# Mixture-of-experts stage: the up-weights of each tile come by SyncE's DMA, not by a GpSimd copy

## What is computed

```python
aff = x @ centroids.T                    # 8 experts
eid = argmax(aff)                        # one expert for each token
alpha = sigmoid(sum(x * centroids[eid]))
xln = norm(x) * ln_g[eid] + ln_b[eid]
h   = relu(xln @ w1[eid] + b1[eid])      # 128 -> 512, the up-weights
y   = h @ w2[eid] + b2[eid]              # 512 -> 128, the down-weights
out = x + alpha * y                      # then x + layernorm(out)
```

## Time and profile before

| | us |
|---|---|
| runs shown | 2639.48, 2630.18, 2635.62 |
| their median | 2635.62 |
| the profiled execution, device time | 2626.78 |
| the profiled execution, span of its instructions | 2625.0 |
| mean granted TensorE clock | 0.88 |

### The profile page before, as it was taken

The page is one execution under the profiler, slowest core; times in us unless marked ns, Lnnn a source line. Parts: engine busy times, 40 slices in busy tenths (PEclk is TensorE's granted clock), DMA queues, the critical chain, the costliest instruction groups (busy, mean ns, idle before and its releaser), DMA issues. The chain is left out here.

```text
span 2625.0 us, 38988 instructions
## 1 busy us (share of the span) xinstructions
PE 1928.0 (73%) x11612; PEld 985.5 (38%) x11693; DVE 1798.8 (69%) x3789; ACT 1524.6 (58%) x2831; POOL 1166.7 (44%) x734
## 2 busy tenths in 40 slices
PE   2688888788787762988267778787877886578886
PEld 0344545455454431888122222222222221133432
DVE  5565655665655432455259999999999999756665
ACT  1576667766676531665256666666676665344453
POOL 1021212212222011466258898998999888500000
PEclk7799989998999865999689999999999888778887
DMA  3010001000010000221111121111121211001111
GB/s 136 9 29 21 25 23 37 22 21 23 24 33 17 13 21 28 59 69 57 52 45 47 49 60 45 44 44 48 49 59 49 55 41 33 25 28 40 32 40 48
DMA packets 137132, 105.23 MB, mean 40 GB/s; under 512 B 12896, under 2 KB 130832, under 8 KB 136608
## 3 DMA queue, kind: packets, MB, share of 16 engines
q1 hardware_dynamic: 131488, 89.51, 12.3%
q0 software_dynamic: 5504, 13.90, 1.5%
HBM read 42.20 MB, written 27.61 MB: 27 GB/s over the span
## 5 line engine op out<-in xcount | busy, mean ns | idle before, releaser
L1843 POOL TENSOR_TENSOR hc<-h,c_rep 128x1024 f32<-128x1024 f32 x256 | 614.4, 2418 | 102.2 <-DVE h L1804 97.4
L1804 DVE TENSOR_TENSOR_SCAN h<-decay,bank 128x1024 f32<-128x1024 f32 x256 | 572.7, 2269 | 0.0
L1689 ACT ACTIVATE decay<-bank,neg_a_r 128x510 f32<-128x510 f32 x512 | 322.8, 683 | 274.0 <-PE bank L1580 241.9
L1795 DVE TENSOR_TENSOR bank<-bank,b_rep 128x1024 f32<-128x1024 f32 x256 | 302.8, 1215 | 45.2 <-PE bank L1567 45.0
L1567 PE MATMUL bank<-u,sel_u 128*128 128x512 bf16 x489 | 166.3, 421 | 209.1 <-DVE h L1804 199.3
L664 ACT ACTIVATE es<-bank 128x384 f32<-128x384 f32 x512 | 210.9, 501 | 127.2 <-PE bank L469 127.2
L1013 POOL DMA_INDIRECT rows_in_dram<-row,idx x64 | 66.5, 1039 | 428.2 <-DVE row L956 413.5
L444 PE MATMUL bank<-xt,w_a 128*128 128x512 f32 x224 | 145.2, 743 | 66.1 <-DVE rot_b L822 31.8
L1567 PEld LDWEIGHTS bank<-u,sel_u 128*128 128x128 bf16 x512 | 32.8, 99 | 385.6 <-DVE h L1804 347.8
L1580 PE MATMUL bank<-d,sel_u 128*128 128x512 bf16 x481 | 166.8, 423 | 4.0 <-issue 1.0
L1594 PE MATMUL bank<-hc,y_sel 128*32 128x512 f32 x1024 | 142.6, 630 | 4.6 <-POOL hc L1843 4.6
(11 more groups left out here) (341 smaller groups left out, 4351.6 us busy)
## 6 DMA issues: line engine op xcount, KB each, us to landing
xvs<-xv SPq DMA_DIRECT2D x16, 512.0 KB, 3.3
xs<-rows_in_dram SPq DMA_DIRECT2D x72, 68.0 KB
w<-in_w_dram SPq DMA_DIRECT2D x2, 2048.0 KB
x_in<-in_x_dram SPq DMA_DIRECT2D x16, 256.0 KB
xlb_dram<-xl SPq DMA_DIRECT2D x16, 256.0 KB
xlb_m<-xlb_dram SPq DMA_DIRECT2D x16, 256.0 KB
x_m<-in_x_dram SPq DMA_DIRECT2D x16, 256.0 KB
g_xn<-yx_dram SPq DMA_DIRECT2D x16, 256.0 KB
```

The lines of the kernel that those rows point to most:

```text
L1689: act.activation(decay[n % 4][:, i, :, 1:], seq(DL[i])[:, :, 1:], ACT.Exp, scale=c["neg_a_r"][:, hf, g:g + 1]).then_inc(s["n_da"], 1)
L1795: dve.tensor_tensor(pair_of(BD[n % 2]), pair_of(BD[n % 2]), b_rep[p if n < NS else q][:, :].unsqueeze(1).to_broadcast([P, 2, STEP]), ALU.m ...
L1804: dve.tensor_tensor_scan(flat(h[n % 4]), decay[n % 4].rearrange("p i b t -> p (i b t)"), BD[n % 2], 0.0, ALU.mult, ALU.add).then_inc(s["n_ ...
L1843: pool.tensor_tensor(hc[n % 4][:, :, :], h[n % 4][:, :, :], c_rep[p][:, :].unsqueeze(1).to_broadcast([P, 2, STEP]), ALU.mult).then_inc(s[" ...
```

## The change

`copy` moves from GpSimd's program to SyncE's, where it is a DMA from SBUF to SBUF. The single semaphore `weights`, which GpSimd raised by 1, is replaced by four, one for each slot, raised by 16 by a DMA; TensorE waits for 16(n+1) of the slot's own. SyncE's order is new as well: the rows of pass 0, the weights of pass 0, the rows of passes 1 to 5, and then one block for each pass k with the four weights of pass k+1 (each behind its wait for `hidden`) followed by the rows of pass k+4 (behind `y2` at k-1).

```diff
@@ block.sync
-            for m in range(ROWS):
-                load(m, m)
-            with sp.Fori(0, PASSES // ROWS - 1) as n:
-                for i in range(ROWS):
-                    done = sp.snap(n * ROWS + (i + 1))
-                    sp.wait_ge(s["y2"], done)
-                    load(n * ROWS + (ROWS + i), i)
+            def copy(n, j, first):
+                t = n * SLOTS + j
+                col = sp.value_load(c["tile_col"][0:1, 0, bass.ds(t, 1)], min_val=0, max_val=(E - 1) * F)
+                if not first:
+                    done = t - (SLOTS - 1)
+                    sp.wait_ge(s["hidden"], done if isinstance(done, int) else sp.snap(done))
+                sp.dma_start(w1[j][:, :], c["w_1"][:, bass.ds(col, F)]).then_inc(weights[j], 16)
+
+            def one_pass(k, x):
+                for j in range(SLOTS):
+                    copy(k + 1, j, False)
+                if x is not None:
+                    done = k - 1
+                    sp.wait_ge(s["y2"], done if isinstance(done, int) else sp.snap(done))
+                    load(k + 4, x)
+
+            load(0, 0)
+            for j in range(SLOTS):
+                copy(0, j, True)
+            for m in range(1, ROWS):
+                load(m, m)
+            one_pass(0, None)
+            one_pass(1, None)
+            with sp.Fori(0, (PASSES - 6) // ROWS) as n:
+                for i in range(2, 2 + ROWS):
+                    one_pass(n * ROWS + i, (i + 4) % ROWS)
+            for k in range(PASSES - 4, PASSES - 1):
+                one_pass(k, None)
@@ block.tensor, up()
-                pe.wait_ge(s["weights"], t + 1)
+                pe.wait_ge(weights[j], 16 * n + 16)
@@ block.gpsimd
-                pool.tensor_copy(w1[j][:, :], c["w_1"][:, bass.ds(col, F)]).then_inc(s["weights"], 1)
...
-                    if main and not is_last(k):
-                        copy(k + 1, j, False)
...
-            for j in range(SLOTS):
-                copy(0, j, True)
```

More of the change, by code:

```diff
@@ L1148, in experts @@
         s = semaphores(nc, ctx, "expert", """loaded0 loaded1 loaded2 loaded3 loaded4 loaded5 sent0 sent1 sent2
-            xn x_t xt_sb xl weights hidden relu_sb result passed w_passed
+            xn x_t xt_sb xl weights0 weights1 weights2 weights3 hidden relu_sb result passed w_passed
             o o_st mv mv2 ln rs nm on y2 y2_st xno""")
@@ L1165, in experts @@
         hold = sb("e_hold", [P, 2])
+        weights = [s[f"weights{j}"] for j in range(SLOTS)]
         loaded, sent = [s[f"loaded{n}"] for n in range(ROWS)], [s["sent0"], s["sent1"], s["sent2"]]
```

## The result

| | kernel before | with the change |
|---|---|---|
| runs, median | 2632.9 (4 runs, 2622.27 to 2639.48) | 2663.52 (4 runs, 2657.82 to 2667.95) |
| profiled execution, device time | 2626.78 | 2657.82 |
| its span | 2625.0 | 2655.7 |
| mean granted TensorE clock | 0.880 | 0.876 |

The ratio is 1.0119, with a 95% interval of 1.0078 to 1.0160: 31 us (20.5 to 42) slower. The forecast was 21 us and 2656.6. Wherever a ratio stands here, the microseconds beside it are the ratio's share of the median of the kernel before; the difference of the two medians can be some us larger. L1204 is the new weight DMA on SyncE.

What follows compares the result with a forecast made beforehand. TensorE was taken to bound passes before scatters, and afterwards a chain through the scatter's delay of its reports. 16.7 + 1.7 + 3 + 0.1 - 0.5 = 21 us on 2635.6 gave 2656.6 us, range 2640 to 2672.

Steps and rivals of the forecast that it cites:

- What bounds the kernel now: Expert stage: TensorE bounds passes before scatters; afterwards the scatter delays TensorE's reports, some 2.7 us a pass, copies not involved.
- Rival (a): Steady passes: the scatter's hold goes with the copies, passes fall from 11.67 to 9.0 us, 2622 us in all; chance 0.08.
- Start stall: Pass 1's first up product starts 16.7 us later, its weights queued on SyncE behind 24 row DMAs and pass 0's weights.
- Clock: Behind the start stall TensorE resumes at its lower clock level and loses 1.7 us, ends 0 and 3.
- SyncE in the steady passes: Passes that scatter and load rows: eight DMAs instead of four make SyncE lag, costing 3 us, ends 0 and 10.
- GpSimd's and VectorE's gain: Expert stage: removing 72 copies from GpSimd frees VectorE's L1386 and L1403; 0.5 us gained, ends 0 and 8.5.
- Rival (b): Expert stage: VectorE's freedom pays the start stall back, within 0.3%, 2643 us; chance 0.10.
- Rival (c): Steady passes: SyncE becomes the bound at 13.0 us a pass without slack, +33 us, 2669 us; chance 0.14.
- Rival (d): Steady passes: the weights' 1 MB a pass of DMA traffic lengthens the scatter by 39 us, 2693 us; chance 0.06.
- The sum: Whole kernel: stall, clock, SyncE's steady load and TensorE's waits less the gain, 21 us slower; ends +7 and +31.

Runs made afterwards that it cites:

- the run with twice the bytes: Kernel before, with SyncE bringing two of four weight slots from pass 3 on, each DMA writing its weights twice: 2635.24 against 2634.19 us, ratio 1.0007.
- the last four runs: The change with SyncE's loop unrolled (ratio 1.0071), the same again (1.0081), SyncE's work in order of need (1.0053), and that with the scatter in twos (1.0042).

## Why the prediction came out as it did

- **What bounds the kernel now: right.** The hold comes from the scatter and not from the copies: it is in the profile after, unchanged, without a copy. In the kernel before, a copy between the indirect DMAs shortens it and takes 1.8 to 2.2 us off a pass. Rival (a) is refuted.
- **Start stall, 16.7 us (15.5 to 18.2): right.** 16.4 measured. Its steps hold too: weights asked for at 1074.10 (forecast 1074.2) and used at 1076.50 (1076.8), with 2.4 us from issue to use against an estimate of 2.6.
- **Clock, 1.7 us: right in size.** The first tile behind the stall took 3.88 us (1076.50 to 1080.38) and the next 2.21, so 1.7 us were lost at the lower clock. The first scatter is 17.7 us later in all, so some 0.4 us was made good. Only this start, run alone, cost 18.4.
- **SyncE in the steady passes, 3 us: the step that failed.** The mechanism was right, and the range (0 to 10) just held it, but the term measured 9.8 us in the trace and 10.5 when run alone. Three sizes were off. The blocks came 12.1 to 12.5 us apart in seven of eleven, near the low end of 12.1 to 13.0, but where the loop turns 2.8 us came on top (3.68 - 0.84), which I had not counted; the mean was 12.69, which makes 11.2 us of lag. The free time was too large: my own figures, 13 less 8.6 to 10.6, give 2.4 to 4.4 us and not 3 to 5, and 11.2 of lag less 9.8 lost leaves some 1.4 (an estimate). With that, the term's upper end would have been near 12 and not 10. And I took weights that come a little late to cost less than their lateness, because TensorE runs ahead of ScalarE. The rows say the opposite: TensorE waited 8.1 us for weights in seven places, and the passes lost 9.8. The six waits of 0.8 to 1.8 us stand each at the head of a pass (scatter to scatter) of 13.0 to 14.0 us, the wait of 0.4 at the head of one of 11.3. Why there are just these two lengths is not shown; two long ones exist before the change as well. The pass between scatters, 12.42 us, came out just above the 11.5 to 12.3 that I had expected and below the 12.8 at which I would have been wrong.
- **GpSimd's and VectorE's gain, 0.5 us: right as far as can be seen.** The relief is in the lines, and in the time there is nothing that could be told from noise. The 44.6 us, my upper estimate from the lock rule of the Trainium skill, "SBUF — State Buffer", Who interferes with whom, did not come. That what the copies held up was VectorE's time to spare fits its idle time in the earlier trace rows, and is argued.
- **Rival (b)**, within 0.3%, is refuted: nothing paid the stall back.
- **Rival (c)** was at 13.0 us a pass, +33: near the measured +31, by its mechanism at a smaller size (12.42 us) over 13 passes. The truth lies between my forecast and it, and nearer to it.
- **Rival (d), traffic: refuted** by the run with twice the bytes.
- **The sum:** 21 forecast, 31 measured. Of the missing 10, 7 are the steady term and 3 lie in later stages; the start came out 0.7 us cheaper than its two terms. The absolute time looks better than that, 2663.5 against 2656.6, and 2.7 us of it is luck: a fourth run moved the median of the kernel before from 2635.6 to 2632.9.

The total could come out within the range only because the large term was a matter of order, which can be counted from two rows. The small one was a matter of slack: I had put it at 3 to 5 us and priced what stuck out too cheaply.

## What to carry to other kernels

When work moves to another engine's queue, write down that queue's order from its first instruction: the first thing that is moved and *also needed early* stands behind everything that was asked for ahead of it, and this cost 17.7 us where the steady load cost 9.8. For the steady load, add the queue's instructions in the stretch where other DMAs slow it, its loop turn included, and compare with the period: at six DMAs a pass there was no cost, at eight there were 10 us. And take work off the engine that holds the chain, not off one that is merely busy: here the same copies, put between the indirect DMAs of the scatter, were worth 25 to 31 us, while the 44 us of copies taken away were worth nothing. Look in the trace whether a moved instruction really ran where it was put: twice the split scatter was split in the program and not in time.

## What the runs showed of the hardware

- Four indirect DMAs of GpSimd in a row held back TensorE's reports to ScalarE and VectorE by 3 to 4.5 us (2.94 and 4.42 in the pass shown) and went with a stretch of SyncE's four row DMAs from 3.86 to 5.5 to 6.2 us in nine of eleven blocks. With a copy of 0.62 us ahead of the third and the fourth the passes fell from 11.67 to 9.87 us, with one between any two to 9.52. The way in which this works is not shown.
- This hold is not a constant. In the last two sessions (the last four runs) the kernel before took 2600 us and not 2633, and four in a row went with passes of 9.4 to 9.75 us. The chip numbered 1 had 2632 us in the first session and 2600 in a later one, so the chip's number does not tell the two apart. The 33 us are about what 13 passes lose at 11.67 us against 9.1; that they are the same thing is argued, not shown. A kernel must be compared with runs of before from the same session, and the gain of the split was measured only where the hold was there.
- A 256 KB DMA from SBUF to SBUF took 494 ns of issue (median), 1.31 us from one to the next inside SyncE's loop ((4.42 - 0.49)/3) and 1.22 before it; 626 ns with twice the bytes. The number of DMAs mattered, their bytes didn't.
- Where the loop of SyncE's program turned, 3.7 to 4.9 us passed between two DMAs in four traces, against 0.8 elsewhere (0.84 in the change).
